# Keys transposed by VectorE and placed by sixteen transfers, in a fused attention and expert kernel

## The reference

```python
def step(state, inp):                       # one chunk of 64 rows
    qq, kk, vv = inp
    inter = jnp.einsum('bhcd,bhde->bhce', qq, state)
    scores = jnp.einsum('bhcd,bhed->bhce', qq, kk) * mask
    intra = jnp.einsum('bhce,bhed->bhcd', scores, vv)
    state = state + jnp.einsum('bhcd,bhce->bhde', kk, vv)
    return (state, inter + intra)
...
x = x + _layernorm(_L0_attn_ref(_layernorm(x), Wq, Wk, Wv, Wo, norm_w))
x = x + _layernorm(_L0_ffn_ref(_layernorm(x), Wg, Wu, Wd, Wr, temperature))
...
gate = jnp.einsum('btd,edi->beti', x, Wg)
up = jnp.einsum('btd,edi->beti', x, Wu)
h = jax.nn.silu(gate) * up
e_out = jnp.einsum('beti,eid->betd', h, Wd)
out = jnp.einsum('bte,betd->btd', weights, e_out)
```

## Time and profile before

| | |
|---|---|
| median of three runs | 1467.39 us (1464.14 to 1468.72) |
| the profiled execution, its own time | 1467.63 us |
| its span in the profile | 1465.9 us |
| TensorE products (PE) | 1443.0 us busy, 98% of the span |
| TensorE weight loads (PEld) | 1254.8 us, 86% |
| VectorE (DVE) | 1027.0 us, 70% |
| ScalarE (ACT) | 613.9 us, 42% |
| GpSimd (POOL) | 428.4 us, 29% |

### The profile page before, as it was taken

How to read it: one execution, slowest core, us unless ns; L and a number is a source line. 1 busy time by engine, 2 the same in 40 slices (tenths; PEclk the granted TensorE clock), 3 DMA queues, 4 the chain that set the end, 5 groups by cost and what they waited for, 6 DMA issues and landing times. The chain is left out here.

```text
span 1465.9 us, 37265 instructions
## 1 busy us (share of the span) xinstructions
PE 1443.0 (98%) x14076; PEld 1254.8 (86%) x14076; DVE 1027.0 (70%) x2459; ACT 613.9 (42%) x1159; POOL 428.4 (29%) x607
## 2 busy tenths in 40 slices
PE   7899999999999999999999999999999999999997
PEld 6788888888888888888888888888888888888887
DVE  6657768586686767768676686867768676685765
ACT  5443534444343343534344344443434445344432
POOL 1322414134241232414134241232413134241230
PEclk9999999999999999999999999999999999999999
DMA  5210100101001010100101001010100101000000
GB/s 173 73 16 6 32 7 14 29 14 29 0 14 29 14 29 0 34 9 14 29 14 29 0 14 29 14 29 0 31 12 14 29 14 29 0 15 16 1 8 22
DMA packets 106945, 32.53 MB, mean 22 GB/s; under 512 B 83616, under 2 KB 106656, under 8 KB 106912
## 3 DMA queue, kind: packets, MB, share of 16 engines
q1 hardware_dynamic: 106912, 32.08, 9.1%
HBM read 23.60 MB, written 8.39 MB: 22 GB/s over the span
## 5 line engine op out<-in xcount | busy, mean ns | idle before, releaser
L878 ACT ACTIVATE late<-gate_ps 128x512 f32<-128x512 f32 x256 | 153.2, 599 | 282.4 <-PE gate_ps L495 282.3
L495 PE MATMUL down_ps<-w_hi,h_hi 128*128 128x256 f32 x976 | 264.9, 294 | 0.0
L775 ACT ACTIVATE h_hi<-late 128x512 fp32r<-128x512 f32 x256 | 161.6, 631 | 235.5 <-DVE late L1125 235.5
L495 PE MATMUL down_ps<-w_hi,h_lo 128*128 128x256 f32 x976 | 254.4, 283 | 0.0
L1125 DVE TENSOR_TENSOR late<-late,up_ps 128x512 f32<-128x512 f32 x256 | 174.9, 683 | 112.1 <-PE up_ps L495 109.6
L1372 POOL TENSOR_TENSOR rms_in<-rms_in,minus_half 128x16 f32<-128x16 f32 x32 | 93.7, 2928 | 491.5 <-DVE rms_in L1073 491.5
L987 DVE TENSOR_TENSOR h_lo<-late,h_hi 128x512 fp32r<-128x512 f32 x256 | 175.6, 686 | 59.7 <-ACT h_hi L775 59.7
L1147 DVE SCALAR_TENSOR_TENSOR late<-down_ps,route,late 128x256 f32<-128x256 f32 x364 | 158.4, 477 | 82.2 <-PE down_ps L495 79.7
L495 PE MATMUL gate_ps<-ft_hi,w_hi 128*128 128x512 f32 x512 | 202.8, 396 | 1.6 <-ACT late L878 1.5
L495 PE MATMUL gate_ps<-ft_hi,w_lo 128*128 128x512 f32 x512 | 202.8, 396 | 0.0
L495 PE MATMUL up_ps<-ft_hi,w_lo 128*128 128x512 f32 x512 | 199.4, 389 | 0.0
(11 more groups left out here) (185 smaller groups left out, 2381.9 us busy)
## 6 DMA issues: line engine op xcount, KB each, us to landing
xs<-in_x SPq DMA_DIRECT2D x32, 256.0 KB, 2.9
out_rows<-late SPq DMA_DIRECT2D x32, 256.0 KB, 2.2
kz<-in_x SPq DMA_DIRECT2D x240, 32.0 KB, 1.8
late<-in_wg SPq DMA_DIRECT2D x7, 256.0 KB, 3.4
late<-in_wu SPq DMA_DIRECT2D x7, 256.0 KB, 4.5
late<-in_wd SPq DMA_DIRECT2D x6, 256.0 KB, 3.4
var_o<-var_s SPq DMA_DIRECT2D x60, 1.0 KB, 1.8
late<-in_wkv_t SPq DMA_DIRECT2D x1, 512.0 KB, 4.2
```

What stands on the lines that cost most here:

```text
L495: last = nc.tensor.matmul(dst, lhs, rhs, start=n == 0, stop=n == len(terms + low_terms) - 1)
L775: return nc.scalar.activation(dst, src, ACT.Copy)
L878: nc.scalar.activation(h_f[:, m, :], gate_ps[:, :], ACT.Silu).then_inc(silu_ready[0], 1)
```

## The change

From block 1 on TensorE no longer transposes keys. Step `kt` leaves the table, both `kv` steps stand in slot 2 and both `q` steps in slot 4, so that all keys are in `k_sb` earlier. A new step `k_turn` in slot 5 lets VectorE transpose `k_sb` in blocks of 32 by 32 into `rows` (four instructions on 128x256), and `place_keys` lets SP issue 16 transfers from `rows` to the new layout of `kz` (`k_t`), each of 32 partitions by 8 runs of 32 numbers. The scores wait for the count of all 16 (`k_placed`). `place_keys` stands at the head of SP's loop, ahead of `load_x_t`.

In block 0 the keys are still transposed by TensorE, but into `up_ps` and not into banks of `att_ps`; the ones-products are steps of `FIRST_PE` now (those for wkv ahead of the transposes of `x`, those for wq behind them), two identity products stand ahead of them where six did, and VectorE's order there changes with them.

```diff
 STEPS = [
     [("xt", 0), ("xt", 1)],
     [],
-    [("kv", 0), ("q", 0)],
+    [("kv", 0), ("kv", 1)],
     [],
-    [("q", 1), ("kv", 1)],
-    [("keep_x1",)],
-    [("kt", 0), ("kt", 1)],
+    [("q", 0), ("q", 1)],
+    [("keep_x1",), ("k_turn",)],
+    [],
...
-FIRST_PE = [("xt", 0), ("xt", 1), ("kv", 0), ("kv", 1), ("q", 0), ...
+FIRST_PE = [("mean", "wkv"), ("xt", 0), ("xt", 1), ("mean", "wq"), ("kv", 0), ("kv", 1), ("q", 0), ...
-FIRST_DVE = [("x_stats", 0), ("x_stats", 1), ("x_norm", 0), ("centre", "wkv"), ("x_norm", 1), ("centre", "wq"),
-             ("low", "wkv"), ("scale", "wo"), ...
+FIRST_DVE = [("x_stats", 0), ("x_stats", 1), ("x_norm", 0), ("x_norm", 1), ("centre", "wkv"),
+             ("low", "wkv"), ("centre", "wq"), ("scale", "wo"), ...
...
-        kz = sb("kz", [P, 2, HG, 2, 2 * P])
-        x_blocks = kz[:, :, :, 1, :]
+        kz = sb("kz", [P, 2, 2, HG, 2 * P])
+        k_t = kz[:, 0, :, :, :].rearrange("p h g c -> p (h g c)").rearrange("p (n c) -> p n c", c=P)
+        k_blocks = rows[:, :, :].rearrange("p t n -> p (t n)").rearrange("p (n c) -> p n c", c=P)
+        x_blocks = kz[:, 1, :, :, :]
...
+            def place_keys(block):
+                reach(sp, k_turned, block, 0)
+                for n in range(P // 32):
+                    for j in range(HPG):
+                        sp.dma_start(k_t[D * j:D * j + D, :, 32 * n:32 * n + 32],
+                                     k_blocks[32 * n:32 * n + 32, :, D * j:D * j + D]).then_inc(k_placed[0], 16)
...
             with sp.Fori(1, BLOCKS - 1) as i:
+                place_keys((i, 0))
                 reach(sp, blocks_turned, (i, 0), 0)
                 load_x_t(i * ROWS + ROWS)
...
+            place_keys((BLOCKS - 1, 0))
             store_out((BLOCKS - 2, 0), (BLOCKS - 2) * ROWS)
...
-                elif kind == "kt":
-                    p = step[1]
-                    reach(pe, k_ready, a, p + 1)
-                    for b in range(B):
-                        for g in range(HG):
-                            last = nc.tensor.transpose(dst[:, g, b * P:b * P + P], k_sb[:, 2 * p + b, g * P:g * P + P],
-                                                       ident[:, :])
...
                     reach(pe, q_ready, a, p + 1 if is_first(a) else HG)
-                    reach(pe, kz_ready, a, p + 1)
-                    if not is_first(a):
+                    if is_first(a):
+                        reach(pe, kz_ready, a, p + 1)
+                    else:
+                        reach(pe, k_placed, a, 0)
                         reach(pe, state_ready, a, 2)
...
-            warm(6)
-            for n, (raw, loaded, columns) in enumerate(((wkv_raw, att_w_loaded[1], 2 * HID), (wq_raw, att_w_loaded[0], HID))):
...
+            warm(2)
...
-                    if not is_first(a):
-                        copy(kz[:, step[1], :, 0, :], src).then_inc(kz_ready[0], 1)
-                        return
...
+                elif kind == "k_turn":
+                    reach(dve, k_ready, a, 2)
+                    for t in range(TILES):
+                        last = nc.vector.transpose(rows[:, t, :], k_sb[:, t, :])
+                    last.then_inc(k_turned[0], 1)
```

More of the change, by code:

```diff
@@ L85 @@
 ]
-FIRST_PE = [("xt", 0), ("xt", 1), ("kv", 0), ("kv", 1), ("q", 0), ("su", 0), ("kt", 0), ("su", 1), ("q", 1), ("kt", 1),
+FIRST_PE = [("mean", "wkv"), ("xt", 0), ("xt", 1), ("mean", "wq"), ("kv", 0), ("kv", 1), ("q", 0), ("su", 0), ("kt", 0), ("su", 1), ("q", 1), ("kt", 1),
             ("s", 0), ("s", 1), ("o", 0), ("o", 1), ("ot", 0), ("ot", 1), ("wo", 0), ("wo", 1), ("ft", 0), ("ft", 1)]
@@ L95 @@
              ("unit", 22), ("ft_whole",), ("unit", 23)]
[L96 to L97 removed]
+FIRST_DVE = [("x_stats", 0), ("x_stats", 1), ("x_norm", 0), ("x_norm", 1), ("centre", "wkv"),
+             ("low", "wkv"), ("centre", "wq"), ("scale", "wo"), ("xt", 0), ("low", "wq"), ("low", "wo"), ("unit", 0), ("xt", 1), ("unit", 1), ("unit", 2), ("unit", 3), ("unit", 4),
              ("unit", 5), ("su", 0), ("unit", 6), ("unit", 7), ("su", 1), ("unit", 8), ("unit", 9), ("unit", 10), ("s", 0),
@@ L111, in psum_steps @@
     return [s for after in steps for s in after
-            if s[0] in ("q", "kv", "kt", "s", "o", "su", "ot", "wo", "ft")] + [ROUTER, ROUTER_T]
-PSUM_STEPS, FIRST_PSUM_STEPS = psum_steps(STEPS), [s for s in FIRST_PE if s[0] != "xt"] + [ROUTER, ROUTER_T]
+            if s[0] in ("q", "kv", "s", "o", "su", "ot", "wo", "ft")] + [ROUTER, ROUTER_T]
+PSUM_STEPS, FIRST_PSUM_STEPS = psum_steps(STEPS), [s for s in FIRST_PE if s[0] not in ("mean", "xt", "kt")] + [ROUTER, ROUTER_T]
 N_PSUM = len(PSUM_STEPS)
@@ L233, in build_program @@
         blocks_turned = counter("blocks_turned", 1)
+        kt_done = sem("kt_done")
+        k_turned = counter("k_turned", 1)
+        k_placed = counter("k_placed", 16 * HPG * P // 32)
         xt_loaded = counter("xt_loaded", 16 * B * KT * P // 32)
@@ L543, in att_step @@
                     last.then_inc(xt_done, 1)
+                elif step[0] == "mean":
+                    n, raw, columns = (0, wkv_raw, 2 * HID) if step[1] == "wkv" else (1, wq_raw, HID)
+                    pe.wait_ge(att_w_loaded[1 - n], 16)
+                    for k in range(KT):
+                        last = nc.tensor.matmul(up_ps[n][:, 0:columns], rz, raw[:, k, :], start=k == 0, stop=k == KT - 1)
+                    last.then_inc(mean_done, 1)
+                elif step[0] == "kt" and is_first(a):
+                    p = step[1]
+                    reach(pe, k_ready, a, p + 1)
+                    for b in range(B):
+                        for g in range(HG):
+                            last = nc.tensor.transpose(halves(up_ps[p][:, :])[:, g, b * P:b * P + P],
+                                                       k_sb[:, 2 * p + b, g * P:g * P + P], ident[:, :])
+                    last.then_inc(kt_done, 1)
                 if step not in PSUM_STEPS:
@@ L550, in att_step @@
                     pass
+                elif is_first(a) and number < 2:
+                    pe.wait_ge(xt_ready[0], number + 1)
                 elif number >= 2:
@@ L594, in att_step @@
                         tok, out_c = 2 * p * P + c, (b * HG + g) * C
-                        last = nc.tensor.matmul(score_banks(p)[C * i:C * i + C, j, out_c:out_c + C], kz[head, p, g, 0, c:c + C],
+                        last = nc.tensor.matmul(score_banks(p)[C * i:C * i + C, j, out_c:out_c + C], k_t[head, 2 * (2 * p + b) + g, C * i:C * i + C],
                                                 q_t[head, g, tok:tok + C], start=True, stop=True)
@@ L604, in att_step @@
                                     last = nc.tensor.matmul(dst[C * i:C * i + C, r, (4 * b + n) * C:(4 * b + n) * C + C],
-                                                            kz[half, p, g, j, c:c + C], q_t[half, g, tok:tok + C],
+                                                            kz[half, j, p, g, c:c + C], q_t[half, g, tok:tok + C],
                                                             start=True, stop=True)
@@ L820, in att_step @@
                 elif kind == "kt":
-                    if not is_first(a):
-                        copy(kz[:, step[1], :, 0, :], src).then_inc(kz_ready[0], 1)
-                        return
+                    act.wait_ge(kt_done, step[1] + 1)
                     for j in range(2):
-                        last = nc.scalar.activation(kz[:, step[1], :, j, :], src, ACT.Copy, scale=odd_even[:, j:j + 1])
+                        last = nc.scalar.activation(kz[:, j, step[1], :, :], halves(up_ps[step[1]][:, :]), ACT.Copy,
+                                                    scale=odd_even[:, j:j + 1])
                     last.then_inc(kz_ready[0], 1)
```

1 line of the change is left out of this document (removed).

## The result

The changed kernel takes 1514.51 us (median), the kernel before beside it 1467.36 us. The ratio is 1.0321, with a 95% interval of 1.0298 to 1.0343: slower by 47 us, where 11 us less had been forecast. One of the changed kernel's four executions took 1744.34 us at a mean granted clock of 0.753, and the ratio leaves it out. The profiled execution took 1514.85 us.

A forecast was written before the change was run, and what follows sets the result against it. TensorE, busy 98% of the span and without gaps in the loop, was taken to bound the kernel. Sum: 1467.6 - 13.2 (transposes) + 1.5 (new wait) + 0.5 (block 0) = 1456.4 us; range 1451 to 1476.

The forecast's parts named there:

- What is removed, 15 x 0.88 = 13.2 us: TensorE, slot 6, blocks 1 to 15: without the key transposes each block saves 0.88 us, 13.2 us in all.
- Four transposes on VectorE cost nothing: VectorE behind low_hidden(2, 0): 1.42 us of key transposes, covered by a 1.34 us wait for TensorE's up; cost nothing.
- The moved steps cost nothing: kv 1 to slot 2, q 0 to slot 4: hidden(2, 0) starts 0.4 us later, hidden by a 2.70 us wait; nothing.
- The new wait, 15 x 0.1 us: TensorE before the scores, slot 10: waits for the last of 16 key transfers, 0.1 us a block, 1.5 us in all.
- item 2 of that chain: SP's key transfers: fifteen distances between issues at 0.495 us each, 7.42 us, with 0.658 us as the upper bound.
- Rival A: Key transfers on SP go out 0.658 us apart, TensorE waits 2.31 us before each block's scores: 1489.6 us; chance 0.18.
- Block 0, +0.5 us between -2 and +2: First block, reordered: an earlier start against more work at half clock level; 0.5 us added, bounds -2 and +2.

The follow-up runs named there:

- turn3: The changed kernel with k_turn moved from slot 5 to slot 3; 1456.22 us, ratio 0.9928 to the kernel before.
- swap_only: The kernel before with only both kv steps in slot 2 and both q steps in slot 4; 1465.36 us, ratio 1.0001.
- busy_wait: The changed kernel with 22 unused transposes of the identity on TensorE in the wait before the scores, from block 1 on; 1496.49 us.
- turn4: The changed kernel with k_turn moved from slot 5 to slot 4; 1458.69 us, ratio 0.9939 to the kernel before.
- patterns: The experiment on forms: the changed kernel with its sixteen key transfers replaced by four forms, four of each, differing in memories and strides; one execution took 1499.85 us.

## Why the prediction was wrong

1. *What is removed, 15 x 0.88 = 13.2 us.* Right. `turn3` turns the loop in 87.36 us where it took 88.23, 0.87 less, and is 11.0 us faster in all by the medians, 12.4 by the two profiled executions. What is between that and 13.2 is within the spread of single executions and was not taken apart.
2. *Four transposes on VectorE cost nothing.* Right: 1.42 us, and `hidden(2, 1)` starts 0.01 us behind them.
3. *The moved steps cost nothing.* Right: `swap_only`, with VectorE's 1.74 us wait for GpSimd where I had named it. The delay was mis-sized: against the scores of its block `hidden(2, 0)` starts 1.1 us later and not 0.4 (705.78 to 721.22 in `swap_only`, 707.33 to 723.86 before). The 2.70 us behind it hid that too.
4. *The new wait, 15 x 0.1 us.* Wrong, and it is item 2 of that chain that failed: the distance between issues. I took 0.495 us from the transfers of `x`, as shape and run length agree, over the 0.658 of the only SBUF to SBUF rows, whose shape differs. The experiment on forms shows that the memories decide and not the shape, so the row to trust was `place_var`. The distance measured is 0.663 us. The landing took 2.0 us, not 1.8, a small second miss. Together 2.5 us of wait in the block read, 2.7 in the mean of all fifteen, where I charged 0.1. Rival A had this mechanism with its right place and distance, 2.31 us of wait, and I gave it 0.18.
5. *What is not in any case: the clock.* Even rival A, with a distance of 0.658 us where 0.663 was measured, gives 1489.6 us, 25 us too few. It takes a wait as so much time lost. Of the 25, about 5 are longer waits (40.1 against 15 x 2.31 = 34.7), 18.0 are the clock, by `busy_wait`, and 1.2 are block 0, which took 1.7 us more in this profile and not 0.5; what is left, 0.6, is the difference between the remainder of 18.6 and the 18.0 measured. I wrote that each microsecond of delay is one of kernel time; here 40.1 us of waits cost 58. The term that failed here is one that the sum put at nothing without a reason: what a wait does to the clock behind it.
6. *Block 0, +0.5 us between -2 and +2.* Inside its bounds, and not to be told from nothing.

The rule that I weighed, on the fixed part of a transfer (the Trainium skill, "DMA: Bandwidth & Descriptors", the section on the anatomy of one DMA: about 2.0 us, given there for GpSimd's path), gave the better figure for the landing on SP's queue: the trace has 2.0 us. The other rule, in the section "Rules for kernel authors" of the same page of the Trainium skill, is to coalesce small transfers. No run did that. The trace shows that the 16 transfers overlap; what adds up is the issuing, 0.66 us each.

The expected gain is there to be had: `turn3`, one line of the table away from the change, takes 1456.2 us, 11 us (0.7%) less than the kernel before and 58 us less than the change. That this is 0.2 us from the 1456.4 forecast for the change is in part luck: the forecast held 1.5 us of waits that `turn3` doesn't have. The gain is small but clear of the noise: the ratio's interval is 0.9911 to 0.9944, and 0.9915 to 0.9941 when it was measured again.

## What to carry to other kernels

Where a new wait is forecast to end close to its need (here 0.14 us ahead, and it came 2.5 us behind), don't rely on the forecast: the step should be moved until the worst row in the trace still leaves room; here one slot earlier (`turn4`) left 0.4 us of waits in all, two slots (`turn3`) none. For the price of a transfer, take the row whose source and destination memories match, ahead of one whose shape matches. And a wait put into a stream of matmuls that had no gap can cost more than its length (here 58 us for 40), since the clock may fall behind it: price both, or fill the wait.

## What the runs showed of the hardware that I had not expected

- A transfer with SBUF on both sides keeps the issuing queue 0.61 us, 0.65 to 0.68 us from issue to issue; one from HBM of the same shape and into the same strided layout 0.45 us and 0.55. Two queues issue such transfers side by side, four in 2.60 us on ScalarE while SP issues twelve in 8.15.
- After 2.5 us without work TensorE's clock fell from 2.4 to 1.2 GHz behind some of the waits and not behind others of the same length (0.55 and 1.00 in the two stretches above), behind 10 of 15 in all. The 40.1 us of waits brought 18 us of loss by the clock with them. With waits of 32.7 us in all (`patterns`) the mean clock was 0.989, with none (`turn3`) 0.995.
- VectorE can be held up by GpSimd. In the trace of before the product `kinds<-kinds,guarded` starts 0.18 us behind the start of GpSimd's addition of the output rows and takes 1.19 us: it ends 0.08 us behind the addition. In `swap_only`, where the addition comes after it, it takes 0.22 us in all 16 blocks; in the trace of before 1.19 in the median. In `turn3` it comes ahead too:

```profile
703.44 1.29 POOL L414 TENSOR_TENSOR late<-late,shared 128x512 f32<-128x512 f32 x1 [3.95 <-ACT shared L781]
```

```profile
703.62 1.19 DVE L1183 TENSOR_TENSOR kinds<-kinds,guarded 128x64 f32<-128x64 f32 x1
```

```profile
697.33 0.23 DVE L1209 TENSOR_TENSOR kinds<-kinds,guarded 128x64 f32<-128x64 f32 x1
```
